# Who adds the output bias of a feed-forward layer to the residual in a three-layer kernel: GpSimd or VectorE

## The reference

```python
x = x + 0.5 * ffn(layernorm(x))
x = x + attn(layernorm(x))
x = x + 0.5 * ffn(layernorm(x))

def ffn(x):                    # per batch element
    probs = softmax(x.reshape(b, -1) @ switch_w.T + switch_b)
    gate, top_idx = top_k(probs, 2)
    h = gelu(einsum(xh, w1[top_idx]) + b1[top_idx])
    o = sum(gate * (einsum(h, w2[top_idx]) + b2[top_idx]))
    return (x + o) @ w3.T + b3

def attn(x):
    q, k, v, a, g = split(x @ w_in.T, 5)          # 16 heads of 32
    q = q * rsqrt(mean(q * q) + eps);  k = tanh(k)
    a = clip(sigmoid(a + 2), 0.6, 0.9995)
    prefix = cumprod(a);  acc = cumsum(k * v / max(prefix, 1e-6))   # in chunks of 64
    y = sigmoid(g) * (q * memory) + (1 - sigmoid(g)) * v
    return y @ w_out.T
```

## Time and profile before

| | |
|---|---|
| median of 3 runs | 547.78 us (547.44 to 548.34) |
| profiled execution | 546.82 us, of which the span of instructions 545.1 us |
| TensorE busy | 490.4 us (90%), mean granted clock 0.966 |
| VectorE busy | 421.5 us (77%), 789 instructions |
| ScalarE busy | 217.2 us (40%) |
| GpSimd busy | 121.8 us (22%), 124 instructions, of them 32 additions of b3 |

### The profile page before, as it was taken

The page is one execution under the profiler, slowest core; times in us unless marked ns, Lnnn a source line. Parts: engine busy times, 40 slices in busy tenths (PEclk is TensorE's granted clock), DMA queues, the critical chain, the costliest instruction groups (busy, mean ns, idle before and its releaser), DMA issues.

```text
span 545.1 us, 8592 instructions
## 1 busy us (share of the span) xinstructions
PE 490.4 (90%) x3204; PEld 354.2 (65%) x3204; DVE 421.5 (77%) x789; ACT 217.2 (40%) x348; POOL 121.8 (22%) x124
## 2 busy tenths in 40 slices
PE   0557996999799999999999999999999938999997
PEld 0544774666578666667766676876667825777775
DVE  3878868799787479987757988767998769878642
ACT  0236651331562322264422237242233529665640
POOL 5140008003001612200180400027211130021220
PEclk9796998999899999999999999999999978999999
DMA  8997004000010200001020001014466142022112
GB/s 342 409 373 307 1 0 156 1 1 0 0 59 0 98 0 1 1 20 40 19 77 0 0 0 38 19 64 187 174 227 254 43 154 81 26 93 76 58 49 86
DMA packets 16370, 48.19 MB, mean 88 GB/s; under 512 B 1232, under 2 KB 1232, under 8 KB 14544
## 3 DMA queue, kind: packets, MB, share of 16 engines
q1 hardware_dynamic: 16336, 47.73, 23.3%
HBM read 39.34 MB, written 8.39 MB: 88 GB/s over the span
## 4 chain that ended last, share of the span: by engine, by line
PE 64%; DVE 18%; issue 8%; SPq 3%; DMA 3%; ACT 2%; POOL 1%; DVEq 0%; POOLq 0%; ACTq 0%
PE bank L435 10%; PE bank L437 9%; PE bank L436 9%; PE bank L740 6%; PE bank L741 6%; PE bank L743 6%; DMA route_w<-in_switch_w 3%; SPq L461 2%; PE bank L612 2%; PE bank L704 2%; DVE kt L1442 2%; PE bank L594 2%; PE bank L707 2%; PE bank L712 2%; PE bank L563 2%
## 5 line engine op out<-in xcount | busy, mean ns | idle before, releaser
L740 PE MATMUL bank<-xh,win_hi 128*128 128x512 f32 x256 | 113.8, 445 | 5.3 <-DVE qn L1419 5.3
L741 PE MATMUL bank<-xl,win_hi 128*128 128x512 f32 x256 | 101.5, 397 | 0.0
L743 PE MATMUL bank<-xbf,win_lo 128*128 128x512 bf16 x256 | 69.9, 386 | 0.0
L1131 POOL TENSOR_TENSOR xa<-xa,tables 128x512 f32<-128x512 f32 x28 | 38.4, 1393 | 134.6 <-DVE xnw L1320 71.4
L740 PEld LDWEIGHTS bank<-xh,win_hi 128*128 128x128 f32 x256 | 48.9, 191 | 21.8 <-DVE qn L1419 5.8
L741 PEld LDWEIGHTS bank<-xl,win_hi 128*128 128x128 f32 x256 | 48.8, 191 | 10.3
L1142 POOL TENSOR_TENSOR rs<-ms,neg_half 128x16 f32<-128x16 f32 x16 | 46.8, 2950 | 29.5 <-DVE ms L1414 29.5
L435 PE MATMUL bank<-w_hi,z_hi 128*128 128x512 f32 x124 | 50.1, 404 | 0.0
L437 PE MATMUL bank<-w_hi,z_lo 128*128 128x512 f32 x124 | 48.5, 391 | 0.0
L436 PE MATMUL bank<-w_lo,z_hi 128*128 128x512 f32 x124 | 48.5, 391 | 0.0
L1136 POOL TENSOR_TENSOR rstd<-mv,neg_half 128x1 f32<-128x1 f32 x16 | 9.6, 598 | 163.6 <-DVE mv L1384 163.6
(11 more groups left out here) (213 smaller groups left out, 1060.7 us busy)
## 6 DMA issues: line engine op xcount, KB each, us to landing
route_w<-in_switch_w SPq DMA_DIRECT2D x14, 512.0 KB, 13.8
route_w<-in_switch_w SPq DMA_DIRECT2D x5, 1024.0 KB, 4.5
xa<-in_x SPq DMA_DIRECT2D x4, 1024.0 KB, 5.1
route_w<-in_switch_w SPq DMA_DIRECT2D x2, 2048.0 KB, 15.4
out<-x SPq DMA_DIRECT2D x16, 256.0 KB, 2.0
raw_y<-in_w_in SPq DMA_DIRECT2D x3, 1024.0 KB, 9.9
x_dram<-x1p SPq DMA_DIRECT2D x12, 256.0 KB, 2.0
xa<-x_dram SPq DMA_DIRECT2D x3, 1024.0 KB, 5.8
```

The costliest lines, as they stand in the source:

```text
L740: pe.matmul(bank[:], win_hi[:, c, r, k, :], xh[:, k, :], start=(k == 0), stop=False)
L741: pe.matmul(bank[:], win_hi[:, c, r, k, :], xl[:, k, :], start=False, stop=False)
L743: mm = pe.matmul(bank[:], win_lo[:, c, r, k, :], xbf[:, k, :], start=False, stop=(k == KC - 1))
L1131: pool.tensor_tensor(ap, ap, b3_half, ALU.add).then_inc(s_xb, 1)
```

## The change

In rows 0 to 2 the four additions of half b3 to the next element's input move from GpSimd to VectorE, into the place right behind the four normalisations that read the same tile. The order on VectorE makes the wait for the normalisations unnecessary; a wait for the halved b3 comes in. GpSimd keeps its powers. The additions for element 0 and those of the last stage remain on GpSimd.

```diff
@@ -1152,8 +1152,6 @@
             with pool.Fori(0, B - 1) as b:
                 for t in range(NT):
                     q_rstd(b, t)
-                for t in range(NT):
-                    residual_bias(b + 1, t)
                 ln_rstd(b + 1)
             for t in range(NT):
                 q_rstd(B - 1, t)
@@ -1320,6 +1318,13 @@
                     ve.tensor_scalar(xnw[:, t * D:(t + 1) * D], src[:, t, :], mv[:, bass.ds(row, 1), t, 0],
                                      rstd[:, bass.ds(row, 1), t], ALU.subtract, ALU.mult).then_inc(s_xn, 1)
 
+            def residual_bias(f):
+
+                ve.wait_ge(s_b3, 1)
+                for t in range(NT):
+                    ap = ffn_input(f)[0][:, t, :]
+                    ve.tensor_tensor(ap, ap, b3_half, ALU.add).then_inc(s_xb, 1)
+
             def split_hidden(f, c, read_job):
 
                 src, hi, lo = hid_set(f, c)
@@ -1507,6 +1512,7 @@
                         select(b + 1, b + 1, 1)
                     if c == 1:
                         normalise(b + 1, b + 1)
+                        residual_bias(b + 1)
                     if c == KC - 1:
                         xt_split(b + 1, 0)
```

## The result

The changed kernel takes 543.5 us (median of 4 runs, 543.17 to 543.72) against 548.06 us in the same comparison: ratio 0.9916, 95% interval 0.9899 to 0.9933. A second comparison with five runs of it gave 544.5 against 547.98 us, ratio 0.9937 (0.9923 to 0.9952). So it is faster by 3.5 to 4.6 us; a gain of 3.74 us was forecast, as a time of 544.0 us. Its profiled execution took 543.42 us, of which the span 541.7.

The account below looks back on a forecast made before the run. TensorE was taken as the bound, VectorE mattering only where TensorE waits in `row_end`. Gains of 3.30 us in row 0 and 0.44 in rows 1 and 2 sum to 3.74, from 547.78 to 544.0 us; range 542.9 to 546.5.

Parts of the forecast that it names:

- VectorE: 7.01 to 5.29 us: In rows 0 to 2, VectorE's stretch from first normalisation to the operation behind the clamp shortens by 1.72 us per row.
- The 4.12 us given back: VectorE's normalisations, `y_lo` and clamp, no longer overlapped by GpSimd's additions, take 2.89 us instead of 7.01 in each row.
- the 2.40 paid: Cost on VectorE of the four moved additions in each row, at 0.60 us from start to start.
- Row 0: transposes at 139.76: TensorE's second-column transposes in row 0's `row_end` start 1.72 us earlier than 141.48, after one wait of 1.98 us.
- The clock stays up: 1.58 us: Behind row 0's wait TensorE keeps full clock, so transposes to `hidden` take 3.54 us instead of 5.12.
- Rows 1 and 2: 0.22 us each: TensorE starts the second transposes 0.22 us late there; earlier VectorE work removes that, 0.44 us in both rows.
- its 4.88 us for what row 0 has more: Excess of row 0 over row 1 from `row_end`'s first transpose to first `hidden`: 11.34 against 6.46 us.
- the rest beside the two waits: The 1.59 us of row 0's 4.88 us excess left after waits of 0.61 and 2.68, ascribed to the lower clock.
- The sum: Whole kernel: 3.30 us from row 0 plus 0.44 from rows 1 and 2, 3.74 us gained.
- rival 3: The change moves nothing because something else holds row 0's transposes at 141.48: 547.8 us, chance 0.09.
- Rival 2: VectorE becomes the bound through costly additions or slowness not due to GpSimd: slower, 553.7 to 556.8 us, chance 0.05.
- Rival 1: The clock still falls behind row 0's wait, so the gain is only 2.16 us: 545.6 us, chance 0.33.

Follow-up runs that it names:

- the run without additions: Changed kernel with the b3 additions of rows 0 to 2 left out on both engines (GpSimd does four 128x1 additions): 541.8 us against 547.54 before.
- the run with both engines: Changed kernel, with GpSimd also doing four same-size additions on spare data in each of rows 0 to 2: 553.78 us against 547.54 before.
- The runs with a longer wait: Changed kernel with one or two further VectorE additions on spare data in row 0: 545.04 and 546.43 us against 547.68 before.
- the run with one more addition: Changed kernel with one further 128x512 VectorE addition on spare data behind the four, in row 0 only: 545.04 us against 547.68 before.
- the run with fills: Changed kernel with GpSimd filling a spare tile four times per row (writes, no reads) beside VectorE's additions: 545.17 us against 547.98 before.

## Why the prediction was right

- *VectorE: 7.01 to 5.29 us.* Measured 5.29, with normalisations of 1.83 us to the next start, additions at 0.60 us and the clamp at 0.45. The 4.12 us given back and the 2.40 paid are both right: the run without additions has the stretch of 2.88, and the run with both engines shows that the relief is due to GpSimd's additions.
- *Row 0: transposes at 139.76.* Measured 139.90, and the wait is 2.05 us from the last start (137.85) less the 0.23 of a matmul, 1.82, where 1.98 was forecast (its row shows 1.65, since it counts from the modelled end). VectorE's stretch began 0.14 us later than before (121.16 against 121.02), so the transposes came 0.14 us later than forecast; `in_part` ended 0.30 us later, which shortened the wait.
- *The clock stays up: 1.58 us.* It did, in both profiles of the changed kernel. The runs with a longer wait show that the term had the right size. That it would stay up was in part luck: the prediction called it near even from two rows, gave it 0.53 against 0.33, and in another run a wait that its row gives as 2.06 us met a fall, where the forecast's 1.98 would read about 1.8.
- *Rows 1 and 2: 0.22 us each.* 0.28 each in the profile, 0.6 together in the timed run. The prediction compared row 0 with a window of row 1 that began 0.18 us too early, so its 4.88 us for what row 0 has more should be 11.34 - 6.28 = 5.06. That the rest beside the two waits came to 1.59, next to the clock's 1.58, was therefore chance: from start to start the two waits are 0.85 and 2.63 us more than in row 1 (1.21 and 3.08 against 0.36 and 0.45), which with 1.58 gives 5.06. The sum used the 1.58, which was read separately and is right.
- *The sum.* By the trace's own time `hidden` starts earlier by 3.16 us in row 0 (146.60 to 143.44; 3.30 was forecast), by 3.38 in row 1 and by 3.63 in row 2, against 3.74. The lengths of the heads alone give 3.46 + 0.28 + 0.28 = 4.02 us. The span shrinks by only 3.4, since row 0's head starts 0.30 us later and the last stage took 88.65 us against 88.38, which is inside that stage's own spread. The timed gains, 4.6 and 3.5, lie on both sides.
- *Rivals.* No sign of rival 3. Rival 2's outcome, VectorE slowed until the kernel is slower, was brought about in the run with both engines and costs 6.2 us; its additions took 1.03 us each. Rival 1 was near: one more addition on VectorE brought the fall, at 1.6 us.

## What to carry to other kernels

Work that is moved to GpSimd to spare VectorE may take more of VectorE than it spares, if both read SBUF at the same time: add up VectorE's own operations during GpSimd's (7.01 us for 2.89 us of work here) before counting the helper as free. When work comes back, put it where the engine waits anyway, not on the first free line: the same four additions cost 1.8 to 1.9 us of row 0's head behind the normalisations and nothing that the heads show in two idle places. And look for stops of TensorE that are just long enough to cost it its clock: between the run with one more addition and the changed kernel the wait differs by 0.78 us (2.43 and 1.65), the head by 2.33 (10.21 and 7.88).

## What was not expected of the hardware

Stops of nearly the same length met both outcomes of the clock. In the run with one more addition a wait of 2.43 us was followed by a granted clock of 0.50. In the run with fills the wait was 2.38 us and the clock stayed:

```profile
140.56 0.66 PE L596 MATMUL bank<-ident_r,xnw 128*128 128x128 f32 x4 [2.38 <-DVE yt L1456]
```

```profile
141.50:144.00 2.50, 2.50 (x16) 1.00 0.00 0
```

In the run with both engines' additions a wait of only 2.06 us was followed by a fall within 1.4 us of work:

```profile
137.82 0.47 PE L437 MATMUL bank<-wo_hi,y_hi 128*128 128x512 f32 x1 [2.06 <-DVE y_lo L1466]
```

```profile
139.20:140.80 1.60, 1.60 (x5) 0.50 0.00 0
```

So in these runs, from 2.06 to 2.43 us, the length alone does not decide. The Trainium skill's statement (page "TensorE: Matmul & The Clock Gate", section "The HAM clock gate") that the check runs free of the kernel's start could explain it; no run here tested that by itself. Single waits of 1.60 to 1.84 us at this place (the changed kernel's two profiles, row 0 changed alone, rows 1 and 2 with both engines adding) were each followed by a granted clock of 1.00 in the profiles.
